# Local attention on one core: the second key projection and the key transposes in other places of the turn, and the first copy of the values on ScalarE

## The reference, cut to what matters

```
h = shift_token(x)
q, k, v = split(h @ wqkv, 3)          # to heads, width 64
q = l2norm(q) * qs
k = l2norm(k) * ksc
q, k = rotary_xpos(q, k)              # t*cos*scale + rotate_half(t)*sin*scale
...
bk, bv = (look_around(bk), look_around(bv))   # a window and the one before
sim = einsum('bhwid,bhwjd->bhwij', bq, bk)    # bq is q * 8
attn = softmax(where(mask, -big, sim))
out = einsum('bhwij,bhwjd->bhwid', attn, bv)
x = x + out @ wo
```

## Time and profile before

| what | value |
|---|---|
| median of 3 runs | 1808.42 us (1806.93 to 1810.94) |
| the profiled execution's own time | 1808.97 us |
| its span, first to last instruction | 1807.2 us |
| TensorE busy in the span | 1703.1 us, 94% |
| ScalarE busy | 1418.3 us, 78% |
| VectorE busy | 1013.9 us, 56% |
| GpSimd busy | 454.0 us, 25% |
| granted clock of TensorE, mean | 0.981 of full speed |

### The profile page before, as it was taken

The page is one execution under the profiler, slowest core; times in us unless marked ns, Lnnn a source line. Parts: engine busy times, 40 slices in busy tenths (PEclk is TensorE's granted clock), DMA queues, the critical chain, the costliest instruction groups (busy, mean ns, idle before and its releaser), DMA issues. The chain is left out here.

```text
span 1807.2 us, 66268 instructions
## 1 busy us (share of the span) xinstructions
PE 1703.1 (94%) x28008; PEld 1021.2 (57%) x28008; DVE 1013.9 (56%) x3118; ACT 1418.3 (78%) x2645; POOL 454.0 (25%) x387
## 2 busy tenths in 40 slices
PE   7998899999999999999999978999998879999988
PEld 4784555555555555555555425666663346666633
DVE  4556433333443333344332069999974489999844
ACT  4444799999999999999999947888872368888832
POOL 1115000000000000000000046877720177787300
PEclk9999799999999999999999989999999999999999
DMA  2001211111111111111100031111110001111100
GB/s 62 1 0 43 105 49 49 52 61 45 63 63 50 49 51 63 45 63 63 49 30 31 3 111 28 25 35 35 29 28 12 0 20 33 35 23 32 34 15 35
DMA packets 47416, 73.26 MB, mean 41 GB/s; under 512 B 8400, under 2 KB 38224, under 8 KB 47184
## 3 DMA queue, kind: packets, MB, share of 16 engines
q1 hardware_dynamic: 47184, 69.85, 12.5%
HBM read 21.08 MB, written 2.10 MB: 13 GB/s over the span
## 5 line engine op out<-in xcount | busy, mean ns | idle before, releaser
L685 ACT ACTIVATE x_probs<-x_pss 128x1024 f32<-128x1024 f32 x832 | 806.6, 1021 | 46.3 <-PE x_pss L606 32.6
L620 PE MATMUL x_acc<-x_probs,x_v 128*32 128x256 f32 x6656 | 437.0, 380 | 0.0
L606 PE MATMUL x_pss<-x_qx,x_kx 32*128 32x256 bf16 x9984 | 349.5, 271 | 6.9 <-ACT x_probs L685 1.9
L606 PEld LDWEIGHTS x_pss<-x_qx,x_kx 32*128 32x128 bf16 x9984 | 222.7, 93 | 192.4 <-ACT x_probs L685 174.5
L620 PEld LDWEIGHTS x_acc<-x_probs,x_v 128*32 128x32 f32 x6656 | 206.7, 110 | 92.1 <-issue 5.7
L732 DVE COPY x_vnext<-x_psp 128x128 f32<-128x128 f32 (+1 forms) x199 | 59.3, 298 | 317.4 <-PE x_psp L584 312.2
L1503 ACT ACTIVATE l_prob<-l_neg_sim,l_neg_top 128x128 f32<-128x128 f32 x512 | 198.2, 395 | 6.0 <-DVE l_neg_top L1325 6.0
L949 POOL TENSOR_TENSOR l_turned_half<-l_raw,l_tabB 128x512 f32<-128x512 f32 x128 | 185.9, 1473 | 50.6 <-ACT l_raw L1462 48.2
L661 POOL COPY x_zq<-zT 128x256 f32<-128x256 f32 x15 | 6.0, 400 | 754.9 <-PE x_psp L591 684.3
L1325 DVE CUSTOM_DVE_ANT_0 l_neg_sim<-l_pss,w_window,l_inv_norm 128x128 f32<-128x128 f32 x512 | 149.0, 347 | 5.7 <-issue 5.0
L959 POOL TENSOR_TENSOR l_direct<-l_direct,l_turned_half 128x1024 f32<-128x1024 f32 x64 | 151.5, 2367 | 0.0
(11 more groups left out here) (201 smaller groups left out, 2617.1 us busy)
## 6 DMA issues: line engine op xcount, KB each, us to landing
x_kx<-x_kp SPq DMA_DIRECT2D x96, 208.0 KB, 2.3
x_cT<-in_context SPq DMA_DIRECT2D x16, 832.0 KB, 4.4
x_qx<-x_qp SPq DMA_DIRECT2D x48, 192.0 KB, 2.3
l_vmid<-l_vt SPq DMA_DIRECT2D x64, 128.0 KB, 2.3
xT<-in_x SPq DMA_DIRECT2D x8, 256.0 KB, 5.7
shifted<-zT SPq DMA_DIRECT2D x32, 64.0 KB, 2.0
hs<-zT SPq DMA_DIRECT2D x32, 64.0 KB, 2.0
out_x<-xT SPq DMA_DIRECT2D x8, 256.0 KB, 2.0
```

The source lines that it names most:

```text
L606: ins = pe.matmul(pss[bank(k, 2 * p + r // 2)][:, r % 2, e, :], kx[par][rows, g, j * P:(j + 1) * P], qx[par][rows, g, a * S:(a + 1) * S], ...
L620: ins = pe.matmul(acc[32 * r:32 * r + 32, 0:S], v[:, j, g, r, :], probs[SLOT[p]][r // 2][:, r % 2, e, :], start=(u == 0), stop=(u == UNITS ...
L685: act.activation(probs[SLOT[p]][y][:, :, :, :], pss[bank(k, 2 * p + y)][:, :, :, :], ACT.Sigmoid, scale=HD ** -0.5).then_inc(weighed, 1)
```

## The change

Four things are moved.

- TensorE: `project_k(x+2, 1)` goes from behind `turn_over(x, 0, 0)` to directly behind `project_q(x+2, 1)`. `flip_k(x+1, 0)` goes ahead of `project_out(x-1)`.
- ScalarE: `copy_k(x+2, 1)` goes from behind the second `copy_out` to directly behind `copy_q(x+2, 1)`, ahead of `copy(x-1, 1, 0)` and `roots(x+1)`.
- VectorE: `multiply_k(x+2, 1)` goes from behind `mask(x, 1, 1)` to directly behind `inverse_norms(x+1)`.
- The copy of the first half of the values goes from the end of VectorE's turn to ScalarE, ahead of `copy_q(x+2, 0)` of the following turn. VectorE keeps that of the second half.

```diff
@@ TensorE, turn
                 project_q(later(x, 2), 1)
+                project_k(later(x, 2), 1)
                 value(later(x, -1), 0)
...
                 turn_over(x, 0, 0)
-                project_k(later(x, 2), 1)
+                flip_k(later(x, 1), 0)
                 project_out(later(x, -1))
-                flip_k(later(x, 1), 0)
@@ VectorE
-            def copy_v(x, t):
+            def copy_v(x):
                 if exists(x):
                     n, r, _ = x
-                    dve.wait_ge(v_projected, 2 * n + t + 1)
-                    at_least(dve, valued, 2 * n - 2)
-                    dve.tensor_copy(vt[r % 2][:, t, :], psvy[:, :]).then_inc(v_ready, 1)
+                    dve.wait_ge(v_projected, 2 * n + 2)
+                    dve.tensor_copy(vt[r % 2][:, 1, :], psvy[:, :]).then_inc(v_ready, 1)
@@ VectorE, turn
                 inverse_norms(later(x, 1))
+                multiply_k(later(x, 2), 1)
                 mask(x, 1, 0)
                 sums(later(x, 2), 0)
                 mask(x, 1, 1)
-                multiply_k(later(x, 2), 1)
...
                 sums(later(x, 2), 1)
-                copy_v(later(x, 1), 0)
                 mask(later(x, 1), 0, 0)
@@ ScalarE
+            def copy_v(x):
+                if exists(x):
+                    n, r, _ = x
+                    act.wait_ge(v_projected, 2 * n + 1)
+                    at_least(act, valued, 2 * n - 2)
+                    act.activation(vt[r % 2][:, 0, :], psvy[:, :], ACT.Copy).then_inc(v_ready, 1)
@@ ScalarE, turn
                 copy(later(x, -1), 0, 1)
+                copy_v(x)
                 copy_q(later(x, 2), 0)
...
                 copy_q(later(x, 2), 1)
+                copy_k(later(x, 2), 1)
                 copy(later(x, -1), 1, 0)
                 roots(later(x, 1))
...
                 copy_out(later(x, -1), 1)
-                copy_k(later(x, 2), 1)
```

More of the change, by code:

```diff
@@ L1351, in turn @@
                 multiply_k(later(x, 2), 0)
-                copy_v(x, 1)
+                copy_v(x)
                 mask(x, 0, 1)
@@ L1417, in _ @@
             norm(before, 1, 1)
-            copy_v(LAST, 1)
+            copy_v(LAST)
             mask(LAST, 0, 1)
```

## The result

| | before | changed |
|---|---|---|
| median of 5 runs | 1808.42 us (1806.93 to 1811.99) | 1819.14 us (1815.21 to 1820.87) |
| profiled execution, its span | 1808.97, 1807.2 us | 1815.21, 1813.4 us |
| granted clock, mean | 0.981 | 0.982 |
| settled turn | 16.33 us | 16.55 us |

The ratio is 1.0064, 95% interval 1.0047 to 1.0082. The kernel became slower, which was forecast, but by 10.7 us and not by 3.9: 0.6 us beyond the upper end of the range.

A forecast was written before the change was run, and what follows sets the result against it. It took a settled turn to be set by a chain over GpSimd, from `inverse_norms` through `scale_keys` to VectorE's product. Terms: 5.3 - 1.1 (turn 0) - 0.3 (turn 14) = +3.9 us, 1812.3 us on the median; range 1806.5 to 1818.5 us.

The forecast's parts named there:

- 0.48 late, less 0.27 of slack, 0.21 late at `inverse_norms`: Settled turn: the moved key copy delays ScalarE's roots 0.48 us; after slack, VectorE's `inverse_norms` starts 0.21 us late.
- GpSimd's chain of 4.64 passes it on: Settled turn: GpSimd's 4.64 us from `inverse_norms` to the second `scale_keys` end is unchanged, ending at +13.41, not +13.20.
- the product ends 0.57 after the scaling: Settled turn: VectorE's `norm(x, 0, 1)` product, held by GpSimd, starts 0.13 us before `scale_keys` ends and needs 0.69 us.
- term of 5.3 us for 25 turns: Settled turns of both layers: each gets 0.21 us longer, charged in 25 turns, 5.3 us in all.
- value copy at 0: Settled turn: moving VectorE's first value copy to ScalarE gains 0, bounds 0 and 0.31 us, and costs ScalarE 0.
- Absorbed: Rival, chance 0.20: the product's 0.23 us is a sharing surcharge; turn stays 16.33 us, sum -1.4 us, 1807 us.
- Missed gap: Rival, chance 0.05: `norm(x, 1, 0)` misses its gap between two GpSimd L949, 1.1 us in 25 turns, +27, 1836 us.
- Slower by the whole copy: Rival, chance 0.08: VectorE's queue has no slack before the roots, so all 0.48 us a turn arrives; 1819 us.
- faster, because VectorE is the bound: Rival, chance 0.15: unloading VectorE lets the mask's 0.31 us reach the end of 26 turns; 9.4 us less, 1799 us.
- Only these 26 turns, and the few beside them, are touched: Scope: turns 1 to 13 of both layers and few beside them change; the rest of 1808.97 us stands outside.
- the product meets `scale_keys` instead: Turn 0, first layer: the product no longer falls behind L949's start, ending about 1.2 us earlier; 1.1 us gained.
- `floor_of` to be held to +6.31: Settled turn: VectorE's `floor_of`, coming at +6.01, waits for GpSimd's `turn_halves`; not being held would show the forecast wrong.

The follow-up runs named there:

- e8: Kernel before with only ScalarE's roots moved one place later, behind `copy_out`: ratio 1.0020 to the kernel before, settled turn 16.55 us.
- e4: Changed kernel with ScalarE's roots ahead of its copy of the second half's keys, as before: ratio 0.9989 to the kernel before, settled turn 16.33 us.
- e7: Changed kernel with ScalarE's roots one place later still, behind `copy_out`: 1826.1 us, ratio 1.0099 to the kernel before, settled turn 17.04 us.
- e1: Kernel before with only the first half's value copy moved from VectorE to ScalarE: ratio 1.0005 to the kernel before, settled turn 16.33 us.
- e2: Kernel before with only the key moves, VectorE still copying both halves of the values: ratio 1.0057 to the kernel before, settled turn 16.55 us.
- e3: Changed kernel with VectorE's sums ahead of the second key product in the two turns before the first: ratio 1.0031 to the kernel before.
- e5: Changed kernel with the edits of e3 and e4 together: ratio 0.9994 to the kernel before, settled turn 16.33 us.
- e9: e5 with VectorE placing first keys ahead of its product and a small unneeded GpSimd product before the first scaling: ratio 1.0076 to the kernel before.

## Why the prediction was wrong, and where it was right

**Right, to the hundredth: the settled turn.** The steps "0.48 late, less 0.27 of slack, 0.21 late at `inverse_norms`", "GpSimd's chain of 4.64 passes it on" and "the product ends 0.57 after the scaling" gave 16.54; it is 16.55. e8 shows the lag alone makes it, e4 that its removal undoes it, e7 that the law goes on. Of the term of 5.3 us for 25 turns, 4.8 fell on turns 2 to 13 of both layers, and these gave 5.0. The value copy at 0 is right (e1). Three rivals fall with these runs. "Absorbed": the product took 1.14 us and ended where GpSimd let it, so its surplus is a hold and no fixed surcharge. "Missed gap": the second product kept its 0.69 us. "Slower by the whole copy" named 1819, the time that was measured, but by 0.48 us a turn; a turn got 0.22 longer, so that the number agrees is chance.

The rival "faster, because VectorE is the bound" is refuted by e4 and e1. The Trainium skill (Perfetto Trace Analysis, section Optimizing Scalar/DVE Operations) says that offloading to ScalarE may make sense where VectorE is saturated. Here VectorE was full but not last, and the offloaded copy was worth nothing: 16.33 us a turn with it and without it (e1).

**The step that failed: "Only these 26 turns, and the few beside them, are touched".** The sum has a term for turns 0 and 14 of those beside them and none for the prelude. The prelude runs the same four `turn` functions with most steps left out, so an engine's order meets other partners there: in the loop `multiply_k` fills a gap, in the prelude it makes ready sums start 0.86 us later, behind a copy of ScalarE's, and TensorE, idle for longer, then needs 1.68 us for a projection of 1.12. The roots, behind `copy_k`, wait for the projection that follows it (e4). The ledger has +3.7 us for the prelude, as much as the whole forecast. Of these, about 1.9 go with the order (e2, e7, against the mean of the kernel before); about 1.8 came with a lower clock in the first layer, whose cause is open. e3's -4.4 against the changed kernel's trace holds both.

**A term with the wrong sign: turn 0, "the product meets `scale_keys` instead", -1.1.** I took the 1.77 us of the earlier trace rows and the projection at half clock for a property of the kernel. The second execution of the kernel before has neither; turns 0 and 1 cost it 67.1 us and not 69.8. Against the mean of both, the changed kernel needs 1.9 us more there, against a forecast of 2 x 0.21 - 1.1. Why it is 1.9 is not settled: with the roots late alone (e8) these turns take 68.1 us, with the keys' moves and the roots first (e4, e5) 68.4 and 68.6, with the keys' moves and the roots late 69.3 (e3) to 70.4 (e2, both executions of the changed kernel).

**Small ones.** Turn 14 gained 1.1 us in both layers, not 0.3; e2 shows it belongs to the key moves and e1 that it does not belong to the value copy, as I had it. Row 16 does not exist, so the only key move with work in turn 14 is `flip_k` ahead of `project_out`. In the kernel before TensorE makes the transposes behind the output projection, and VectorE waits for them:

```profile
1326.28 0.60 PE L1053 MATMUL l_psk<-w_identity,l_direct 128*128 128x128 f32 x4
...
1326.92 0.69 DVE L1258 COPY l_kT<-l_psk 128x512 f32<-128x512 f32 x1 [0.66 <-PE l_psk L1053]
```

In e2 this wait is gone. The first mask was to start at +1.21 and `floor_of` to be held to +6.31. The mask starts at +1.48, 0.32 us after the scores and not 0.04. The hand-over from TensorE to VectorE is not slow, as the two rows above show (1326.88 to 1326.92); but ahead of the mask VectorE's sequencer has three small instructions of its own (L1319 and twice L869, register work and waits, not counted as busy), in the trace at 1200.36, 1200.45 and 1200.53. So `floor_of` comes at +6.32 by itself and nothing of a hold shows, which the prediction had named as a sign of being wrong. The result, 0, was the same for another reason. And the hold's 0.57 us in turn 0 came from halving the record of a pair; where a record stands alone it is 0.54 to 0.56.

Added up: forecast +3.9; the missing prelude +3.7, turns 0 and 1 +2.6 (1.9 instead of -0.7), turn 14 -0.8, turns 2 to 13 +0.2 (5.0 instead of 23 x 0.21) make +9.6, against the +9.5 of the ledger. The range failed for the same reason: its upper end was built from errors of the settled turn, none of the prelude. That +9.6 meets +9.5 so closely is arithmetic, since the parts were measured from the same ledger.

## What to carry to other kernels

Walk a change of order through the turns before the first and after the last as well, where the steps that covered it are missing; a hand-written turn is tuned for the full loop only. An engine that is busy 98% of a turn need not be its bound: look for an instruction that gets longer when it is asked for earlier, and find who lets it go. Take an odd row near a start or a change of stage for an event until a second execution shows it again.

## What the runs showed of the hardware that I had not expected

- The hold between GpSimd and VectorE is the same for all three forms of GpSimd instructions here (L949, L959, L968): the product ends 0.54 to 0.56 us after the end of their record, in the eight cases of six kernels shown here (the kernel before in the earlier trace rows), and so do all 546 products of over 0.76 us in the fourteen traces. This agrees with the exclusive lock of the Trainium skill (SBUF — State Buffer, section SBUF: two separate sides). What was new is how sharp the edge is. Where one GpSimd instruction follows another without a pause, its record starts 0.04 us before the other's ends; a product whose record starts ahead of it goes next, one that starts with or behind it waits for the whole next instruction. In all traces 0.08 us before the end was early enough and 0.04 was too late. In e9 the two fell 0.13 us apart in the rows shown, and its turns alternated between 16.44 and 17.64 us.
- A product of 8 elements a row on GpSimd (128x8) has a record of 0.20 us and moved the next instruction by 0.16:

```profile
1178.47 0.20 POOL L970 TENSOR_TENSOR l_idle<-l_inv_norm 128x8 f32<-128x8 f32 x1 [2.20 <-DVE l_inv_norm L1313]
...
1178.63 1.04 POOL L971 TENSOR_TENSOR l_direct<-l_direct,l_inv_norm 128x512 f32<-128x512 f32 x1
```

- TensorE's results reach VectorE 0.04 us after the modelled end of the transposes (1326.88 to 1326.92), as they reach ScalarE. In front of the mask it is 0.32 us (1200.31 to 1200.63), with the three sequencer instructions in between.
- Nearly the same code outside the local attention took 1271.4 to 1280.9 us from one execution to the next. A difference of a few microseconds in one profiled execution has to be looked for stage by stage, as the ledger does: the first profiles of the two kernels differ by 6.2 us in their spans (1807.2, 1813.4), the medians by 10.7.
